# One product of 3840 columns in place of three of 1280 in the typed passes of a graph network

## What is computed

```python
# layer 0
A = edge_emb[edge_type].reshape(-1, MSG_DIM, HID_DIM)
msg = jnp.einsum('emh,eh->em', A, h_src)
m = jax.ops.segment_sum(msg, edge_dst, num_segments=n_nodes)
...
# layer 2, run twice
for r in range(NUM_RELATIONS):
    msg = msg + jnp.where((edge_type == r)[:, None], x_src @ W[r], jnp.zeros((), x.dtype))
cnt = jnp.zeros((num_nodes, NUM_RELATIONS), x.dtype).at[dst, edge_type].add(1.0)
norm = 1.0 / jnp.maximum(cnt[dst, edge_type], 1.0)
agg = jax.ops.segment_sum(msg * norm[:, None], dst, num_segments=num_nodes)
```

## Time and profile before

| | |
|---|---|
| median of 3 runs | 15562.0 us (15555.02 to 15573.69) |
| the profiled execution | 15625.38 us, of which the span is 15623.6 us |
| DVE busy | 12468.0 us (80%) |
| PE busy | 11688.2 us (75%) |
| POOL busy | 8206.3 us (53%) |
| the expansion's products (L1292) | 3537 found, 2787.5 us, 850 ns each |
| `e0` | about 5.4 to 6.6 ms of the span |
| `e2`, `e3` | about 9.1 to 10.3 ms and 10.4 to 11.5 ms |

### The profile page before, as it was taken

How to read it: one execution, slowest core, us unless ns; L and a number is a source line. 1 busy time by engine, 2 the same in 40 slices (tenths; PEclk the granted TensorE clock), 3 DMA queues, 4 the chain that set the end, 5 groups by cost and what they waited for, 6 DMA issues and landing times. The chain is left out here.

```text
span 15623.6 us, 474073 instructions
## 1 busy us (share of the span) xinstructions
PE 11688.2 (75%) x158466; PEld 9184.0 (59%) x158467; DVE 12468.0 (80%) x23402; ACT 7727.0 (49%) x17320; POOL 8206.3 (53%) x8491
## 2 busy tenths in 40 slices
PE   1344444444444388789999978878959999999998
PEld 1233333333333266578888856656648888888886
DVE  4577777777777588878888878878868999999997
ACT  2244444444444366556666646656635555555554
POOL 1777777777777799711111179989951111111111
PEclk9855555555555699999999989999989999999998
DMA  8233333333333377622222267767752222222222
GB/s 225 63 91 90 92 91 91 91 91 91 91 91 91 110 220 220 186 98 109 103 109 105 107 170 225 225 189 226 226 130 80 82 84 82 85 84 82 84 85 65
DMA packets 1742381, 1897.00 MB, mean 121 GB/s; under 512 B 1011017, under 2 KB 1449883, under 8 KB 1716987
## 3 DMA queue, kind: packets, MB, share of 16 engines
q1 hardware_dynamic: 1617117, 1853.32, 40.1%
q0 software_dynamic: 123008, 41.82, 1.7%
q10 hardware_dynamic: 2078, 0.15, 0.0%
HBM read 1445.12 MB, written 449.46 MB: 121 GB/s over the span
## 5 line engine op out<-in xcount | busy, mean ns | idle before, releaser
L637 POOL DMA_INDIRECT rec<-sort_ring,sort_idx x3712 | 3657.0, 985 | 1657.0 <-issue 1129.3
L1292 DVE TENSOR_TENSOR e_full<-e_feats,e_masks 128x1280 bf16<-128x1280 bf16 x3537 | 2787.5, 850 | 244.8 <-ACT e_feats L1249 218.1
L1192 PE MATMUL e_acc<-e_full,e_sel 128*128 128x384 bf16 (+1 forms) x11760 | 2120.4, 327 | 360.1 <-DVE e_full L1292 360.1
L1444 PE MATMUL e_acc<-e_outer,e_sel 128*128 128x272 f32 x7840 | 1896.1, 397 | 3.9 <-DVE e_outer L1539 3.9
L1247 ACT CAST e_masks<-e_kind 128x1280 bf16<-128x1280 fp8e4 x1179 | 1482.8, 1258 | 775.4 <-DVE e_full L1292 737.2
L753 PE MATMUL sort_ps_rows<-ident_h,sort_code 128*128 128x128 f16 x7840 | 1067.5, 308 | 1036.7 <-DVE sort_code L879 862.3
L1159 POOL TENSOR_SCALAR e_lo<-iota_b,e_src_lo 128x128 bf16<-128x128 bf16 x1470 | 1683.7, 1145 | 0.0
L1192 PEld LDWEIGHTS e_acc<-e_full,e_sel 128*128 128x128 fp8e4 x11760 | 1061.0, 97 | 1023.2 <-issue 387.0
L900 DVE TENSOR_SCALAR sort_made<-sort_rows_code,code_of 128x1664 fp8e4<-128x1664 f16 x882 | 1642.9, 1935 | 0.0
L1444 PEld LDWEIGHTS e_acc<-e_outer,e_sel 128*128 128x128 f32 x7840 | 1458.7, 190 | 282.0 <-issue 4.1
L1158 POOL TENSOR_SCALAR e_hi<-iota_b,e_src_hi 128x98 bf16<-128x98 bf16 x1470 | 1521.2, 1035 | 68.4 <-POOL e_src_lo L1154 64.1
(11 more groups left out here) (455 smaller groups left out, 27113.4 us busy)
## 6 DMA issues: line engine op xcount, KB each, us to landing
e_hot<-stream SPq DMA_DIRECT2D x888, 480.0 KB, 3.7
stream<-sort_made SPq DMA_DIRECT2D x98, 2568.0 KB
e_sel<-stream SPq DMA_DIRECT2D x1176, 160.0 KB, 2.5
e_st<-stream SPq DMA_DIRECT2D x99, 1888.0 KB, 7.3
sheaf_gather<-stream SPq DMA_DIRECT2D x393, 384.0 KB, 3.1
e_hot<-stream SPq DMA_DIRECT2D x294, 448.0 KB, 3.5
tail<-sort_made SPq DMA_DIRECT2D x98, 660.0 KB
sheaf_by_dst<-tail SPq DMA_DIRECT2D x491, 128.0 KB, 3.0
```

The lines of the kernel that those rows point to most:

```text
L637: nc.gpsimd.indirect_dma_start(out=rec[q], out_offset=bass.IndirectOffsetOnAxis(ap=idx[:, s, q, c:c + 1], axis=0), in_=ring[:, s, q, c, :] ...
L1192: last = mm(acc[h][:, 0:cols_all], now[:, n * P:(n + 1) * P], full[q & 1][:, n, :], start=j == 0, stop=j == NT - 1)
L1292: last = v.tensor_tensor(full[q & 1][:, :, 0:cols].rearrange("p j (t k f) -> p j t k f", t=TYPES, k=3)[:, :, :, k, :], feats[q & 1][:, :, ...
L1444: last = mm(acc[h][:, 0:cols], sel[q & 1][:, n, :], outer[q & 1][:, n, :], start=j == 0, stop=j == NT - 1)
```

## The change

`expand` makes the 3840 columns in one product. `feats` is read with a repeat over the types, `masks` with a repeat over the three parts, and the result is the same values in the same places. The cast in `e0`, the waits and the semaphore increments stay as they are. Nothing changes on the other engines.

```diff
@@ -1282,17 +1282,15 @@
-                    shape = [P, BATCH, TYPES, D]
+                    shape = [P, BATCH, TYPES, 3, D]
                     dve.wait_ge(taken, b * BATCHES + q + 3)
                     dve.wait_ge(added, b * BATCHES + q + 1)
                     dve.sem_inc(dve_passed, 1)
                     if count:
                         v.tensor_copy(full[q & 1][:, :, cols:cols_all], kinds)
-                    for k in range(3):
-                        last = v.tensor_tensor(full[q & 1][:, :, 0:cols].rearrange("p j (t k f) -> p j t k f", t=TYPES, k=3)[:, :, :, k, :],
-                                               feats[q & 1][:, :, k:k + 1, :].to_broadcast(shape),
-                                               masks[q & 1][:, :, :, :], ALU.mult)
-                    last.then_inc(expanded, 1)
+                    v.tensor_tensor(full[q & 1][:, :, 0:cols].rearrange("p j (t k f) -> p j t k f", t=TYPES, k=3),
+                                    feats[q & 1][:, :, :, :].unsqueeze(2).to_broadcast(shape),
+                                    masks[q & 1][:, :, :, :].unsqueeze(3).to_broadcast(shape), ALU.mult).then_inc(expanded, 1)
```

## The result

The changed kernel takes 15950.0 us, median of 4 (15937.13 to 15962.23), against 15561.97 (15555.02 to 15573.69): 1.0248 times the time before, 95% interval 1.0235 to 1.026, 388 us more. The forecast was 16000 and slower.

The account below looks back on a forecast made before the run. DVE's path over PE and ACT bounded the kernel; after the edit POOL's 11 jobs a block would. Passes add 128 + 163 + 171 = 462 us, less 24 of lead: +438 on 15562, so 16000; range 15,700 to 16,250.

Parts of the forecast that it names:

- the ring from X1 over PE and ACT to X0: Path of a block: 5.55 us from one expansion (X1) to the next block's (X0), the other two (X2, X3) inside.
- DVE's ring alone: Block time after the edit if POOL did not set it: 12.0 - 0.3 = 11.7 us in e2 and e3.
- the rival of the lost rate: DVE's product falls out of the double rate and takes 4.14 us, giving 18,400 us; chance 0.03.
- POOL's wait grows with the product, twice for a comparison: POOL waits inside its instruction until DVE's running product ends; a comparison reads column and table, so it waits twice.
- The count of jobs: POOL's 11 jobs a block, fitted beside products or into free time, give blocks of 13.7 us in e2 and e3.
- the rival that its error repeats: The job count, 0.7 us too long on the kernel before, errs so again: sum 231 us, 15,790; chance 0.12.
- G: Time of a block in which DVE runs no products, needed for POOL's remaining jobs: 5.24 us in e2 and e3.
- One job fewer: POOL's pair of casts falls beside products, each waiting 2.07 us: block 14.25 us, +570 us.
- no growth of the wait: Rival: POOL's wait stays or its jobs find other gaps; only DVE's saved starts count, 97 us less, 15,465; chance 0.11.
- PE's clock: Rival: PE, idle longer, drops to the lower clock; a quarter of the blocks so gives 16,570 us; chance 0.06.
- One short and one long in turn: Sign to look for: blocks of 13 to 14 us, perhaps alternating, since a late POOL set shifts the next block's expansion.
- the 63 us between the profiled execution and the median: Last step: the median of runs lies 63 us (0.4%) under the profiled execution, so 16063 became 16000.

Follow-up runs that it names:

- pool1_one: The changed kernel with one pair of POOL's comparisons a block in place of five and one histogram matmul; 15472.75 us, 0.9935 times the kernel before.
- one_read: The changed kernel with a constant in place of the column in POOL's comparisons of the typed passes; 15664.08 us, 1.0053 times the kernel before.
- e2: Not a run: one of the kernel's three typed passes; a block takes 12.04 us in the kernel before, 13.39 in the changed kernel.
- e3: Not a run: another of the kernel's three typed passes; a block takes 11.96 us in the kernel before, 13.33 in the changed kernel.

## Why the prediction was right, and where its sizes were off

- **What bounds the kernel.** Right: the ring from X1 over PE and ACT to X0, with X2 and X3 inside it. pool1_one shows its length, 11.50 us a block, where the forecast for "DVE's ring alone" said 11.7. DVE's idle time before X0 grew from 0.98 to 1.33 us, as told (about 1.4).
- **The product.** 2.158 us against 2.15; the rival of the lost rate is out.
- **POOL's wait grows with the product, twice for a comparison.** Right, the step that carried the sign. Up to 4.5 us were measured where 4.2 was said (two products of 2.07, and I had left out the comparison's own time beside them). The reading of two waits was tested by one_read.
- **The count of jobs.** The blocks came out too long, as the prediction itself suspected. It gave 13.7 for `e2` and `e3`, and 13.39 and 13.33 were measured; for `e0` 13.6 against 13.10. That is 343 us where 438 were summed, and lies between the count (438) and the rival that its error repeats (231). The jobs were counted right: 3 beside products and 8 free were said for `e2`, 3.1 and 7.9 were found (4 and 7 in `e0`, as said). The term at fault is G, the free time that the free jobs need, 5.24 and 4.70 us. It puts every free job wholly into time without a product. But one that begins shortly before a product ends beside it without waiting, as that of 9702.59 does (0.60 us, with X0 at 9702.97); in `e2` this is so at 155 of 194 rows of products. The parts so hidden sum to 0.32, 0.29 and 0.28 us a block in `e0`, `e2` and `e3`, where the forecast was 0.50, 0.31 and 0.37 too long; the rest is open. In the kernel before they are 0.34 and 0.38 us in `e2` and `e3`, about half of the 0.7 by which the count was too long there. A comparison that begins only some 0.03 to 0.06 us before the product waits once: 2.50 us.
- **A sum that does not come out.** "One job fewer, 14.25 us, +570": 0.55 us more on 294 blocks is 162, so 600. The range holds either.
- **Chances for no growth of the wait (0.11):** refuted by rows of 4.5 us.
- **PE's clock (0.06):** it came, but as a companion of the long blocks. After the wait of 3.80 us scatter 3 took 3.37 us instead of 1.78, and this stretch shows a mean granted clock of 0.75 of 2.4 GHz (0.50, the lower level, from 9704.6 to 9711.4); the next, 1.00:

```profile
9700.00:9713.40 13.40, 9.60 (x103) 6.38 (x100) 5.43 (x7) 5.45 (x8) 12.90 (x21) 0.75 0.43 129
9713.40:9724.60 11.20, 10.51 (x169) 7.86 (x168) 9.69 (x9) 7.36 (x12) 11.20 (x8) 1.00 0.84 237
```

  How much of the loss is the clock's is open. It lengthens a long block by some 2 us (an estimate from scatter 3, 1.6 us longer, and the gather before it), but those 2 us are also free time for POOL, which then has its lead sooner. No run separates the two with one start. With two starts the clock stayed at 1.00 through `e3`, and the block was still 0.71 us over that of before: POOL's bound needs no clock to cost time.
- **The pattern.** "One short and one long in turn" was told; it is mostly two short ones to a long one.
- **From span to median.** I let the 63 us between the profiled execution and the median stand. After the change they were 12. So the two errors, 95 us too much in the sum and 51 too little in this step, partly cancelled, and 16000 lay only 50 us over the result (the last 6 us are what lies between the passes and the spans): that closeness is in part luck.

## What to carry to other kernels

Fusing small instructions on one engine saves their fixed cost there, but each start is also a turn for another engine that has to wait for them, as POOL did here: look in the trace for instructions of the other engine whose time follows the length of these, and count how many turns its work needs before the next wait falls due. An engine that is 92 to 98% busy with such waits inside its instructions has little slack, even if nothing waits for it now. And the repair is cheap once the cause is known: moving some of that work into idle time of the engine that was waited for turned a loss of 2.4% into a gain of 0.7%.

## What the runs showed of the hardware

- A comparison on POOL waits separately for its column and its table: up to 4.54 us with both in SBUF, up to 2.48 with a constant in place of the column, beside products of 2.16. POOL gets one turn at each product, 4.0 products waited for in each block of four.
- The Trainium skill ("SBUF — State Buffer", Who interferes with whom) tells of a lock on the shared port that blocks the other engine for a whole instruction. These runs agree on the holder's side and add that the one who waits can be made to wait twice in one instruction.
- A comparison of POOL's that began 0.3 us or more before a product ended beside it in its usual 0.5 to 0.6 us (9702.59, with the product at 9702.97).
- DVE's own comparison of the same shape, reading the same table and column, costs 0.16 us from start to start, where POOL's costs 0.54 undisturbed.
- Matmuls after 3.8 us of idle PE ran at the lower clock for more than 3 us (10 matmuls of 384 columns in 3.37 us instead of 1.78; granted clock 0.50, that is 1.2 GHz).
